# Layer-1 and layer-2 counts read back in eighths, and layer 1's dense products six places later, in a three-layer graph network

## What is computed

```python
h = jnp.maximum(_layernorm(x, axis=-1), 0.0)        # x: 6250 x 128, f32
# three layers, widths 128 -> 256 -> 256 -> 128; 206250 edges (100000 both ways, and 6250 loops), sorted by dst
def _mean_agg(x, src, dst, n):
    msg_sum = jax.ops.segment_sum(x[src], dst, num_segments=n)
    cnt = jax.ops.segment_sum(jnp.ones((src.shape[0], 1), x.dtype), dst, num_segments=n)
    return msg_sum / jnp.maximum(cnt, 1.0)
def _sage_conv(x, src, dst, Wl, bl, Wr):
    return _mean_agg(x, src, dst, x.shape[0]) @ Wl.T + bl + x @ Wr.T
h = jax.nn.relu(_batch_norm(_sage_conv(h, src, dst, Wl0, bl0, Wr0), gamma0, beta0))
h = jax.nn.relu(_batch_norm(_sage_conv(h, src, dst, Wl1, bl1, Wr1), gamma1, beta1))
h = _sage_conv(h, src, dst, Wl2, bl2, Wr2)
return x + jax.nn.log_softmax(h, axis=-1)
```

## Time and profile before

| | |
|---|---|
| median of three runs | 1542.47 us (1542.36 to 1542.49) |
| the profiled execution: its time | 1533.44 us |
| its span, first to last instruction | 1531.7 us |
| mean granted TensorE clock | 0.976 |

### The profile page before, as it was taken

One profiled execution on the slowest core, in us unless ns is written; L12 is line 12 of the kernel. 1 busy time (PEld: TensorE's weight loads), 2 busy tenths in 40 slices (PEclk: granted clock), 3 DMA queues, 4 the chain that ended last, 5 costly groups with the idle time before them and its releaser, 6 DMA issues.

```text
span 1531.7 us, 31641 instructions
## 1 busy us (share of the span) xinstructions
PE 1377.2 (90%) x13759; PEld 845.9 (55%) x13759; DVE 558.5 (36%) x1023; ACT 540.8 (35%) x906; POOL 638.5 (42%) x636
## 2 busy tenths in 40 slices
PE   1499999999999999998898898998989899999996
PEld 1377777777777775444444443443547764444444
DVE  6968677777778743100100101010000111222223
ACT  4887868787878847100000000000000340000101
POOL 3422131314131100366666666666663015666640
PEclk9999999999999999999999999999989999999998
DMA  6254444555454435665565565565552378998982
GB/s 159 90 187 163 175 147 177 186 187 187 180 190 176 184 95 199 225 213 177 177 210 183 176 221 173 174 223 168 182 188 91 112 243 298 319 330 287 338 308 76
DMA packets 95107, 297.67 MB, mean 194 GB/s; under 512 B 18928, under 2 KB 54274, under 8 KB 91724
## 3 DMA queue, kind: packets, MB, share of 16 engines
q1 hardware_dynamic: 63132, 225.47, 41.2%
q0 software_dynamic: 25408, 65.24, 13.8%
q10 hardware_dynamic: 6424, 4.88, 1.0%
HBM read 204.30 MB, written 91.22 MB: 193 GB/s over the span
## 4 chain that ended last, share of the span: by engine, by line
PE 70%; another core or an unknown queue 9%; ACT 7%; issue 6%; POOL 4%; DVE 3%; DMA 1%; DVEq 0%; ACTq 0%; SPq 0%
PE bank L1575 24%; PE bank L1157 14%; PE cells L1575 7%; PE cells L1149 7%; POOL hots L518 4%; PE bank L1172 3%; PE bank L1175 3%; ACT ring L654 3%; PE cells L1200 2%; PE bank L1578 2%; ACT junk L602 2%; PE cells L1578 2%; PE bank L1925 1%; PE cells L1656 1%
## 5 line engine op out<-in xcount | busy, mean ns | idle before, releaser
L518 POOL DMA_INDIRECT hots<-table,src_i x518 | 491.8, 949 | 458.8 <-DMA table<-parts 191.5
L1575 PE MATMUL bank<-ring,parts 128*128 128x500 f16 x2058 | 475.4, 379 | 11.6 <-issue 11.0
L654 ACT CAST ring<-cells 128x980 f16<-128x980 f32 (+1 forms) x325 | 335.6, 1059 | 109.1 <-PE cells L1149 96.1
L1575 PEld LDWEIGHTS bank<-ring,parts 128*128 128x128 f16 x2058 | 193.0, 97 | 245.8 <-issue 43.4
L1157 PE MATMUL bank<-ring,parts 128*128 128x250 f16 (+1 forms) x2450 | 320.1, 272 | 2.7 <-ACT ring L654 2.3
L882 DVE TENSOR_TENSOR hots<-iotas,tab 128x980 f16<-128x980 f16 (+3 forms) x262 | 245.4, 994 | 9.6 <-ACT tab L618 9.6
L1157 PEld LDWEIGHTS bank<-ring,parts 128*128 128x128 f16 (+1 forms) x2450 | 216.6, 98 | 35.0 <-ACT ring L654 3.7
L1575 PE MATMUL cells<-ring,parts 128*128 128x500 f16 (+1 forms) x784 | 179.0, 378 | 9.8 <-issue 9.7
L1710 ACT ACTIVATE Z<-bank,vec 128x250 f32<-128x250 f32 x48 | 19.9, 465 | 464.0 <-remote 275.5
L962 DVE BATCH_NORM_STATS2 st<-Z 128x6 f32<-128x250 f32 x96 | 35.5, 411 | 338.2 <-ACT Z L1710 286.3
L1149 PE MATMUL cells<-hots 64*128 64x49 f16 x4670 | 107.3, 186 | 43.0 <-DVE hots L882 31.7
(11 more groups left out here) (205 smaller groups left out, 931.0 us busy)
## 6 DMA issues: line engine op xcount, KB each, us to landing
ring<-c_blocks SPq DMA_DIRECT2D x117, 750.0 KB
c_blocks<-ring SPq DMA_DIRECT2D x25, 3062.5 KB
ring<-c_blocks SPq DMA_DIRECT2D x39, 812.5 KB
rcb<-rc_row SPq DMA_DIRECT2D x68, 125.0 KB
hots<-table,src_i POOLq DMA_INDIRECT x518
Z<-in_x_dram SPq DMA_DIRECT2D x4, 768.0 KB, 7.3
table<-parts SPq DMA_DIRECT2D x2, 1536.0 KB
table<-parts ACTq DMA_DIRECT2D x2, 1536.0 KB
```

The costliest lines, as they stand in the source:

```text
L518: pool.indirect_dma_start(out=got[layer][:, 5 * (r % NGOT) + i, :], out_offset=None, in_=tables[layer], in_offset=bass.IndirectOffsetOnAxi ...
L654: act.copy(blk[c % 2][:, :, :].rearrange("p a (d g) -> p a d g", d=GD)[:, :, :, GPS * i:GPS * i + n], cells[t % 2][:, :, 0:n * NA].rearran ...
L1575: ins = pe.matmul(bank[b][:, 0:2 * BD].rearrange("p (s d) -> p s d", s=2), lhs, ring[0:r, :, BD * a:BD * a + BD], start=(a, part) == (0, 0 ...
```

## The change

Four things. (1) `NPC = 8`: the 49 tiles are cut into eight pieces (from tiles 0, 6, 12, 18, 24, 30, 36 and 42) instead of four, in both layers; every load, every `t_part` and every wait of TensorE for a load follows them. (2) A piece has one semaphore, for both slots (`d_load[k]`), and TensorE waits once per piece. What it waits for is `stands[layer][u]`: for a pair all loads up to its own two; for a single block the count at the end of the layer, so sweep 9 waits also for the same piece of the block of sweep 10. (3) Layer 1's dense products start at place 12 of a sweep (`NA // 4`), not 6. (4) The two other uses of the number four follow (`out_store` in layer 2 stays at the middle of a sweep).

```diff
-    quarters = [(NA * k // 4, NA * (k + 1) // 4) for k in range(4)]
-    quarter_from = {a0: k for k, (a0, _) in enumerate(quarters)}
+    pieces = [(NA * k // NPC, NA * (k + 1) // NPC) for k in range(NPC)]
+    piece_from = {a0: k for k, (a0, _) in enumerate(pieces)}
...
+    stands = [{}, {}, {}]
+    n = 0
+    for layer in (1, 2):
+        for u, js in enumerate(sweeps[layer]):
+            n += 16 * len(js) if u else 0
+            stands[layer][u] = n
+        for u, js in enumerate(sweeps[layer]):
+            if len(js) == 1:
+                stands[layer][u] = n
...
-    for layer, a0 in ((1, NA // 8), (2, NA // 4)):
+    for layer, a0 in ((1, NA // 4), (2, NA // 4)):
...
-        d_load = [[sem(f"d_load{s}{k}") for k in range(4)] for s in range(2)]
+        d_load = [sem(f"d_load{k}") for k in range(NPC)]
...
-            a0, a1 = quarters[k]
+            a0, a1 = pieces[k]
             u = sweep_of[layer][j - 2]
-            if k < 3:
-                sp.wait_ge(t_part, 3 * (sbase[layer] + u) + k + 1)
+            if k < NPC - 1:
+                sp.wait_ge(t_part, (NPC - 1) * (sbase[layer] + u) + k + 1)
             else:
                 sp.wait_ge(t_agg, swept(layer, u))
...
-                         .rearrange("p (a d) -> p a d", d=BD)).then_inc(d_load[slot_of[layer][c]][k], 16)
-
-        def quarter_here(layer, u, k):
-
-            for j in sweeps[layer][u]:
-                c = orders[layer][j]
-                pe.wait_ge(d_load[slot_of[layer][c]][k], ring_in[layer, c])
+                         .rearrange("p (a d) -> p a d", d=BD)).then_inc(d_load[k], 16)
+
+        def piece_here(layer, u, k):
+
+            pe.wait_ge(d_load[k], stands[layer][u])
...
-                for k in range(4):
+                for k in range(NPC):
                     for j in sweeps[1][u]:
                         block_load(1, j, k)
...
-                    if u and k == 1 and len(sweeps[2][u]) == 2:
+                    if u and k == NPC // 2 - 1 and len(sweeps[2][u]) == 2:
                         for i in ends[sweeps[2][u][0]]:
                             out_store(i)
```

More of the change, by code:

```diff
@@ L33 @@
 NGOT = 3
+NPC = 8
 NEAR = 3
@@ L148, in gnn_program @@
         assert all(slot_of[layer][c] == slot_of[layer - 1][c] for c in orders[layer][0:2])
-    ring_in = {}
-    for s in range(2):
-        n = 0
-        for layer in (1, 2):
-            for j, c in enumerate(orders[layer]):
-                if slot_of[layer][c] == s:
-                    n += j >= 2
-                    ring_in[layer, c] = 16 * n
     sweeps = [[], [], []]
@@ L1579, in pe_sums @@
                                     start=(a, part) == (0, 0), stop=(a, part) == (FULL, 1))
-            if part == 1 and a + 1 in quarter_from:
+            if part == 1 and a + 1 in piece_from:
                 ins.then_inc(t_part, 1)
@@ L1750, in pe_layer1 @@
                 for t, a, summed in places(1, u):
-                    if a in quarter_from and summed[0] == 0:
-                        quarter_here(1, u, quarter_from[a])
+                    if a in piece_from and summed[0] == 0:
+                        piece_here(1, u, piece_from[a])
                     for part in summed:
@@ L1950, in pe_layer2 @@
                 for t, a, summed in places(2, u):
-                    if a in quarter_from and summed[0] == 0:
-                        quarter_here(2, u, quarter_from[a])
+                    if a in piece_from and summed[0] == 0:
+                        piece_here(2, u, piece_from[a])
                     for part in summed:
```

## The result

The changed kernel takes **1560.63 us** (median of four runs, 1559.42 to 1561.94); the kernel before took 1542.41 us (four runs, 1541.72 to 1542.49): a ratio of 1.0119, 95% interval 1.0102 to 1.0137. That is 18.2 us slower. The forecast was 1543.5 us, and the time lies above the upper end of the range, 1552.

A forecast was written before the change was run, and what follows sets the result against it. TensorE was taken to bound layer 2, DMA close under it; layer 1 left TensorE 43.7 us idle, its updates hanging. −2.5 + 0 + 5.0 − 1.5 = +1.0 us gave 1543.5 us; range 1534 to 1552.

The forecast's parts named there:

- One semaphore for a piece: Sweep 9, a single block, also waits for sweep 10's load: between 0 and +8.9 us, taken as +5.0.
- the lower end: Sweep 9's added wait costs 0 if sweep 8's update comes at once, the load landing at 1135.7.
- the discount: At sweep 9, waiting 6.3 us lets late updates and GpSimd catch up; +5.0 us taken, under the upper end +8.9.
- rival C: Slower: sweep 9's wait paid in full, products' savings lost to GpSimd's gathers in layer 1; +8 to +10.6 us, chance 0.27.
- Eight pieces: Both layers: extra loads per sweep are hidden, cost 0; halved bursts let gathers land sooner, taken as −1.5 us.
- The cover: Layer 2: smaller packets raise DMA share by at most five points, 0.90 to 0.95, still under TensorE.
- rival D: Half packets slow layer 2's load queue to 17.6 kB per engine-us: +16 us, 1558.5 us; chance 0.04.
- The −1.5 for gathers: Layer 1: halved load bursts shorten TensorE's waits for gathers, between 0 and −4.6 us, taken as −1.5.
- Dense products at place 12: Layer 1: later dense products save 2.5 us in sweep 4; sweep 3 taken as 0, other sweeps nothing.
- the turn takes it over: Sweep 3 of layer 1: the dense product's wait moves to the gathered window's turn, about 3.7 us; net 0.
- What would make it wrong: Sweeps 1 to 8 together changing by more than 6 us, or TensorE standing before any other piece.
- the likeliest case: Whole kernel: the forecast of a small net, +1.0 us, own range 1540.5 to 1546.5 us, chance 0.42.

The follow-up runs named there:

- e2: The kernel before with one semaphore per piece for both slots alone, still four pieces, products at place 6; ratio 1.0071.
- k1: The same kernel as e2, run on a chip whose updates hang, against the kernel before; ratio 1.0067.
- e5: The changed kernel with layer 1's dense products back at place 6; ratio 1.0106 of the kernel before.
- h1: The changed kernel as it is, run once more on another chip beside the kernel before; ratio 1.0106.
- e4: The changed kernel with sweep 10's loads on a semaphore of their own; ratio 1.0049 of the kernel before.
- e1: The changed kernel with sweep 10's loads on their own semaphore and dense products back at place 6; ratio 1.0042 of the kernel before.
- k4: The kernel before with layer 2's first matrix a sweep earlier and layer 1's turns and first rounds up to 8 places later; ratio 1.0016.
- k3: The same kernel as e1, with loads in layer 2's sweep 0 held until quarters would start; ratio 1.0009 of the kernel before.
- h3: The same kernel as e1, with layer 2's first matrix made a sweep earlier; ratio 1.0004 of the kernel before.
- h2: The same kernel as e1, run on another chip whose updates hang; ratio 1.0046 of the kernel before.
- e3: The kernel before with the dense products of layer 1 at place 12 alone; ratio 1.0018.
- h4: The same kernel as e3, run once more on another chip, against the kernel before; ratio 1.0032.
- g6: The same kernel as h3, run on a chip whose updates come at once; ratio 0.9966 of the kernel before.
- k2: The changed kernel with four pieces in layer 2, sweep 10's loads on their own semaphore, products at place 6; ratio 0.9987 of the kernel before.
- m2: The kernel before with layer 2's first matrix made a sweep earlier, nothing else; ratio 0.9986.

## Why the prediction was wrong

**What bounds the kernel** was read rightly for the chips whose updates hang: TensorE in layer 2, late updates in layer 1.

***One semaphore for a piece*, +5.0: the mechanism was right, the term half its size.** The load went out 1.3 us after the update, as taken, and landed 6.15 us after, where 6.3 was taken. What failed is first the lower end, 0 for an update that comes at once. It was reckoned from 1135.68, when TensorE was back in its stride after the crawling; but an update on time leaves no crawling to replace. In the profile of the changed kernel the update came at once, and TensorE stood 7.49 us; in e2 8.96. With it goes the discount: "6.3 us of waiting also let the late updates and GpSimd catch up, and TensorE may crawl less after it". Alone, the shared semaphore costs 0.67% where updates hang and 0.71% where they don't (k1, e2): 10 us both times. So from the update to the landing the wait is paid in full. What a late update adds on top seems not to be: the gaps are then 12.5 (k1), 13.4 (e5) and 15.5 us (h1), and in k1, which has this part alone, the price is 9.8 us all the same. So that much of the discount may be right. The two profiles themselves differ in sweep 9 by just 5.0 us (46.7 against 41.7), but sweep 9 without the wait takes 36.2 (e4) to 42.8 us (e1) from one execution to the next (k4, with other rounds, 51.8), and with it 46.7 to 53.8.

The clock, left to rival C, belongs into the term: 2.5 us in e2. So far rival C had it: its "+8 to +10.6" is this term alone. Its second reason, that GpSimd's gathers pace layer 1, wasn't tried by itself.

The Trainium skill had a rule that speaks against this part and that I left out: one semaphore for each slot in flight, not one for each stream (DMA: Bandwidth & Descriptors, Why a DMA increments its semaphore by 16 and not by 1). It is given for stale data; here TensorE waits for the sum of both loads, so nothing is stale, and the price is time.

***Eight pieces*, "Cost 0" and −1.5: the step that failed.** The cover was right. Over three steady sweeps of layer 2 the counts move at 21.0 kB per engine-us, before at 22.4 (19.51 MB in 79.8% of 72.8 us, 20.01 MB in 76.8% of 72.7): 6% slower and 3 points of share more, within the five that were reckoned. TensorE is busy all of the time in both, so rival D is out. What the prediction set beside D from the Trainium skill (DMA: Bandwidth & Descriptors, Bandwidth and Anatomy of one DMA) is measured there on transfers issued by GpSimd. SyncE's loads show no 16 us a sweep: these three sweeps take 24.1 to 24.4 us each in both kernels.

What the step lacked is another transfer that a finer load is ahead of. Finer pieces don't only end sooner, they start sooner, at other times; at the end of layer 2's sweep 0 that is when the table is stored. The chain is: counts beside the table (gathers 6 us late); the first gathers, one each 1.25 us from 1285.85 to past 1299, then lie over the end of sweep 1 (1297.4); VectorE's mean, which answers sweep 1's updates, comes 6.1 us after the last product instead of 1.5; VectorE's matrix stands behind it, and TensorE waits 7.6 us in place of 3.0. Its first link and its last are tried (k3, h3). That the gathers make the mean late is inferred from the two coming together, in every profile of the slower chips: where the first twelve gathers end after sweep 1 or with it (after, e1, e4, e5, h1, h2, h3), the mean comes 4.8 to 6.7 us after the last product; where they end 3 us or more before it (before, e3, h4, k1 to k4), 0.6 to 1.7. On chip 2 they end 1.0 us after it in g6, and the mean comes after 0.09 us, so the gathers alone don't do it.

Holding the loads back, loading quarters in layer 2 or making the matrix early each take it away (k3, k2, h3). It costs 0.42 to 0.46% (e1, h2), 6 to 7 us, and sweep 2 of layer 2 shows all of it: 33.3 to 34.7 us in the six profiles with eight free pieces and the late matrix (after, e1, e4, e5, h1, h2), 26.6 to 29.2 in the six with four pieces there or held loads (before, e3, h4, k1, k2, k3), 6.6 us less on average. In layer 1 the pieces cost nothing that runs can tell: with place 6, sweeps 1 to 8 take 507.7 to 517.1 us with eight pieces (e1, e5, h2, h3) and 508.4 and 515.2 with four (before, k1). The −1.5 for gathers lies under what chip 2 shows (5.8 to 2.4 us), and doesn't show where updates hang.

***Dense products at place 12*, −2.5: wrong in sign.** What failed is that only sweeps 3 and 4 were reckoned, and the rest put at nothing. Sweep 4 was as said: no gap before the dense product at 823.79. In sweep 3 the turn was to wait 3.7 us; in this execution it didn't, since the update was seen 1.7 us after the product and not 5.2. But "the turn takes it over" holds at other turns: with the product gone from between them, a turn stands 20 products, 4.4 us, behind its window's last round, too near where the round's update takes 9. TensorE and VectorE at the worst of them, in the changed kernel:

```profile
908.99 0.62 PE L1203 MATMUL cells<-hots,tab 128*32 128x512 f16 x5
909.54 4.40 PE L1576 MATMUL cells<-ring,parts 128*128 128x500 f16 x20
919.67 0.69 PE L1212 MATMUL cells<-cf,gsum 128*128 128x128 f32 x2 [5.74 <-issue]
```

```profile
918.62 0.48 DVE L1026 TENSOR_SCALAR gsum<-cells,rcg 128x256 f32<-128x256 f32 x1 [22.53 <-issue]
```

The round is over at 909.6, VectorE acts at 918.62. Before, the same turn came with a dense product between, at 914.48, and didn't wait. I looked at the two sweeps where a product had waited and took the rest as covered. By itself place 12 costs 0.18% and 0.32% (e3, h4), 3 to 5 us; in e4, beside the pieces, 0.07%, which the intervals can't tell from none. The exchange shows in all profiles where updates hang: with place 12 no dense product has a named wait for VectorE's mean, but the turns wait 10.7 to 18.9 us in all (after, e3, e4, h1, h4); with place 6 and the rounds as before the products wait 3.2 to 12.1 us for the mean, the turns 0 to 4.0.

The parts alone make 0.67 + 0.44 + 0.25 = 1.36%, the whole 1.06 to 1.19% (h1, after). That is 21 us against 18.2; the intervals of the parts can't tell whether they overlap.

**What would make it wrong** was named: sweeps 1 to 8 changed by 12.9 us, over the 6. Yet here the sign was no proof. On the chips whose updates hang, those sweeps take 515.9 to 522.0 us in all five kernels with place 12 and 507.7 to 517.1 with place 6 (512.8 on average of eight, 518.7 of the five), so some 6 us of the 12.9 go with the moved products, and the rest is what executions differ by.

**The chances.** C, slower, had 0.27, and the range ended at 1552, below C's far end. The measured time lies nearest to D's 1558.5, by chance: what D describes didn't happen. It was the likeliest case's discount that made the forecast small, and a discount for a wait that would fall into time lost anyway had no row behind it. The chances were also added up slightly wrong: with a ninth of the forecast's spread on either side, slower is 0.36 (0.27 + 0.04 + 0.05) and within 0.2% 0.33, not the other way round. What stays open is why the updates hang, and why on some chips alone.

## What to carry to other kernels

A wait for a transfer that the code makes certain is charged in full, the slow clock behind it included; let it be reduced only where a row shows the cover. When loads are cut finer, list what else is transferred at each of the new issue times, above all small rows that someone waits for at the start of the next stage. And where an engine takes its instructions in order, moving work away from between a producer and its consumer is a change of its own: look at every such pair, not at those which waited before.

## What the runs showed of the hardware

The same kernel takes 1542 us on one chip and 1445 on another, and most of the difference sits where GpSimd issues gathers: sweeps 1 to 8 of layer 1 take 508 us or 447 (before, and m2). On the slower chips (4, 7, 8, and those of the first two measurements) TensorE's updates come late there: in h4 the last product of sweep 7 is over at 1074.0, and SyncE acts at 1085.72, 11.7 us after it. GpSimd waits for such updates; on the faster ones GpSimd's waits in layer 1 are only these (the kernel before with the early matrix, m2):

```profile
POOL hots L518 <- issue: 108.8, 357, 0.3
POOL hots L518 <- DMA table<-parts: 104.1, 1, 104.1
POOL hots L518 <- PE cells L1200: 6.3, 12, 1.7
```

No "remote" is left of its 66.4 us. Chips 2 and 3 are of this kind: in their six profiles every sweep end of layers 1 and 2 but the very last is acted on within 0.04 us. Each of chips 2, 3, 4, 7 and 8 was measured in one group only, so no run separates the chip from the hour. A gather takes as long on both (0.95 us of GpSimd), and so do layer 2's steady sweeps, 24.3 us. So a gain of a few tenths of a percent found on one chip, as eight pieces in layer 1 are on chips 2 and 3, has to be tried on one of the other kind as well.
